# Transformer block with cross-attention and a mixture of experts: seams between stages, and the shared expert's two groups in phases

## The reference

```python
x = x + xattn(_layernorm(x), ctx)     # 16 heads; q, k normalised per head; 496 main keys and
                                      # 16 further keys, each with its own softmax; ctx @ Wo + bo
x = x + moe(_layernorm(x))            # router picks 2 of 7 experts for a row
# every expert, and one shared expert that takes all rows:
u = xt @ Wup + bup
g = silu(u @ Wgate + bgate) * u
out = g @ Wdown + bdown
```

## Time and profile before

| what | value |
|---|---|
| time, median of 3 runs | 1103.38 us (1101.81 to 1104.4) |
| the profiled execution | 1103.13 us; span 1101.3 us |
| PE busy | 976.3 us, 89% of the span |
| ACT busy | 501.8 us, 46% |
| DVE busy | 607.6 us, 55% |
| POOL busy | 686.0 us, 62% |
| mean granted TensorE clock | 0.957 of 2.4 GHz |
| stage project | 0.3 to about 181 us |
| stage attend | 182.5 to 476.4 us |
| stage output | 477.7 to about 633 us |

### The profile page before, as it was taken

One profiled execution on the slowest core, in us unless ns is written; L12 is line 12 of the kernel. 1 busy time (PEld: TensorE's weight loads), 2 busy tenths in 40 slices (PEclk: granted clock), 3 DMA queues, 4 the chain that ended last, 5 costly groups with the idle time before them and its releaser, 6 DMA issues. The chain is left out here.

```text
span 1101.3 us, 17337 instructions
## 1 busy us (share of the span) xinstructions
PE 976.3 (89%) x5217; PEld 443.2 (40%) x5218; DVE 607.6 (55%) x1074; ACT 501.8 (46%) x894; POOL 686.0 (62%) x601
## 2 busy tenths in 40 slices
PE   1789993999999999959988779999999999999898
PEld 1345541222222222226643235544454455554343
DVE  5777773587887877637754323333234333222288
ACT  2466663577877877622242123333333333333340
POOL 1464565479889998742317478989899997000470
PEclk9889996599999999979999889999999999999999
DMA  7135444234343321023426534344334432113674
GB/s 252 34 100 158 118 123 147 72 123 148 130 150 126 115 86 48 20 81 125 134 87 230 199 125 135 116 133 133 112 119 139 143 122 90 57 57 144 240 199 155
DMA packets 89035, 138.26 MB, mean 126 GB/s; under 512 B 9209, under 2 KB 48121, under 8 KB 88593
## 3 DMA queue, kind: packets, MB, share of 16 engines
q1 hardware_dynamic: 74752, 91.07, 25.0%
q0 software_dynamic: 12896, 45.10, 12.4%
q10 hardware_dynamic: 1328, 1.36, 0.4%
HBM read 84.03 MB, written 53.48 MB: 125 GB/s over the span
## 5 line engine op out<-in xcount | busy, mean ns | idle before, releaser
L934 DVE TENSOR_REDUCE nm<-a_psS 128x2 bf16<-128x992 f32 x128 | 152.3, 1190 | 77.1 <-PE a_psS L945 75.6
L871 ACT ACTIVATE p_t<-a_psT 128x512 f32<-128x512 f32 x256 | 143.4, 596 | 36.6 <-PE a_psT L961 34.6
L1716 PE MATMUL e_psU<-w_exp,e_xT 128*128 x456 | 112.6, 383 | 7.5 <-issue 5.7
L1716 PE MATMUL e_psY<-w_exp,e_gT 128*128 x456 | 110.6, 379 | 3.5 <-issue 2.3
L1716 PE MATMUL e_psG<-w_exp,e_uT 128*128 x456 | 110.8, 379 | 2.5 <-DVE e_uT L1683 2.5
L961 PE MATMUL a_psT<-q_stk,k_stk 98*128 98x512 f16 x256 | 101.3, 401 | 5.8 <-ACT p_t L871 5.8
L945 PE MATMUL a_psS<-k_stk,q_stk 96*128 96x512 f16 x256 | 81.7, 402 | 22.7 <-DVE nm L935 13.8
L830 POOL TENSOR_TENSOR p_sum<-p_t,p_t 128x512 f32<-128x512 f32 x64 | 81.3, 1270 | 29.4 <-ACT p_t L871 24.2
L191 POOL TENSOR_TENSOR w_exp<-e_raw,w_exp 128x1024 f32 (+1 forms) x42 | 90.3, 2149 | 6.0 <-POOL e_raw L188 4.5
L1697 DVE TENSOR_TENSOR e_g<-e_g,e_u 128x512 f32<-128x512 f32 x38 | 48.6, 1279 | 80.9 <-ACT e_g L1676 80.9
L833 POOL TENSOR_TENSOR p_sum<-p_sum,p_t 128x512 f32<-128x512 f32 x64 | 81.4, 1272 | 17.0 <-ACT p_t L871 10.7
(11 more groups left out here) (323 smaller groups left out, 1919.1 us busy)
## 6 DMA issues: line engine op xcount, KB each, us to landing
xs_dram<-zero SPq DMA_DIRECT2D x38, 256.0 KB, 5.6
e_x<-xs_dram SPq DMA_DIRECT2D x38, 256.0 KB, 2.7
ys_dram<-e_y SPq DMA_DIRECT2D x38, 256.0 KB, 2.1
q_dram<-q_st SPq DMA_DIRECT2D x24, 256.0 KB, 2.9
k_dram<-k_st SPq DMA_DIRECT2D x24, 256.0 KB, 3.9
q_stk<-q_dram SPq DMA_DIRECT2D x64, 96.0 KB
k_stk<-k_dram SPq DMA_DIRECT2D x64, 96.0 KB
e_raw<-in_L_ffn_Wup_dram POOLq DMA_DIRECT2D x12, 512.0 KB, 4.0
```

Source lines behind the costliest of these rows:

```text
L871: act.activation(probs(w, k), psT[:, k % 2], ACT.Exp, scale=SCALE / (QS * QS)).then_inc(s["exp"], 1)
L934: dve.tensor_reduce(pair[:, :, 0:1].rearrange("p q o -> p (q o)"), psS[:, :, 0:NMAIN], AX.X, ALU.max, negate=True)
L1716: ins = pe.matmul(dst[:, :], stationary, moving, start=(k == 0 and chunks[0] == 0), stop=(k == len(terms) - 1 and chunks[-1] == KD - 1))
```

## The change

It moves work between stages and changes an order; no arithmetic is added or left out.

1. The last pair's six stores of q and k are issued at the head of attend by SP, not at the end of project. `q_st`, `k_st` keep their addresses. ACT, before its first write of split weights (head 8), waits for all stores.
2. After the last head's loads, SP fetches rows 0 to 127 of x and bo (to 128 partitions) into `a_raw`. In output POOL's first instruction adds the two into `x_in[0]`, and ACT's first copies bo into its own tile. `load(0)` and bo's load go away; POOL makes its constants after that addition, and DVE's two copies of them move from before tile 0 to tile 4.
3. ACT's first square root is a dummy one, so the table is loaded at once; the two scalings of the experts' biases go from ahead of tile 0 to behind the square root of tile 4.
4. The shared groups run phase by phase: up 0, up 1, gate 0, gate 1, down 0, down 1 (before: up 0, gate 0, up 1, down 0, gate 1, down 1). `u`, `uT` and `gT` get a second copy, in three quarters of `xT_all` that are free by then; the one that is stored to `xT_dram` has its own semaphore for it, and ACT waits for it before `up(1, 0)`. `prefix` goes from behind gate(0, 1) to behind up(1, 3). DVE does all eight `down` behind the preparation of `pmat`.

In project and attend:

```diff
-            store(sp, B - 1, TB - 1)
...
+            pair = TB // PAIR - 1
+            for buf, dst, done, parts in ((g_["q_st"], q_dram, g_["qk_stored"][0], (0, 0, 1)), (g_["k_st"], k_dram, g_["qk_stored"][1], (0, 1, 0))):
+                for r, part in enumerate(parts):
+                    d = dst[r, (B - 1) * D:B * D, pair * PAIR * P:(pair + 1) * PAIR * P]
+                    sp.dma_start(d.rearrange("(c p) t -> p c t", p=P), buf[:, pair, part]).then_inc(done[pair], 16)
             for u in range(N):
...
+            sp.wait_ge(g_["split_done"], len(early) + 1)
+            sp.dma_start(raw[:, 0, :], t["x"].rearrange("b s d -> (b s) d")[0:P, :]).then_inc(g_["x0_loaded"], 16)
+            sp.dma_start(raw[:, 1, :], t["L0_xattn_bo"].partition_broadcast(P)).then_inc(g_["bo_loaded"], 16)
...
+                    if n == 0 and j == 0:
+                        for q in g_["qk_stored"][0] + g_["qk_stored"][1]:
+                            act.wait_ge(q, 3 * 16 * NT // PAIR // 2)
                     g_["scale_half"](act, raw[:, :, :], raw_ld, n + 1, k, half, m, n, j)
```

In output, SP, POOL and ACT:

```diff
-            load(0)
-            sp.dma_start(bo[:, :], t["L0_xattn_bo"].partition_broadcast(P)).then_inc(s["bo_loaded"], 16)
             load(1)
+            load(2)
             sp.dma_start(wr[:, :, :], t["L0_ffn_Wr"].rearrange("(k p) n -> p k n", p=P)).then_inc(s["r_loaded"], 16)
-            load(2)
...
+            pool.wait_ge(g_["x0_loaded"], 16)
+            pool.wait_ge(g_["bo_loaded"], 16)
+            pool.tensor_tensor(x_in[:, 0], g_["a_raw"][:, 0, :], g_["a_raw"][:, 1, :], ALU.add).then_inc(s["xb_r"], 1)
...
-            act.wait_ge(s["b_loaded"], 16 * 8)
-            act.activation(bias_hi[:, :, :], bias_raw[:, :, :], ACT.Copy, scale=WS).then_inc(s["b_16"], 1)
-            act.activation(bias_16[:, :, :], bias_raw[:, :, :], ACT.Copy, scale=WS).then_inc(s["b_16"], 1)
+            act.wait_ge(g_["bo_loaded"], 16)
+            act.activation(bo[:, :], g_["a_raw"][:, 1, :], ACT.Copy).then_inc(s["bo_copied"], 1)
+            act.activation(sqrt_first[:, :], ident[:, 0:1], ACT.Sqrt)
...
+                if n == TB:
+                    act.wait_ge(s["b_loaded"], 16 * 8)
+                    act.activation(bias_hi[:, :, :], bias_raw[:, :, :], ACT.Copy, scale=WS).then_inc(s["b_16"], 1)
+                    act.activation(bias_16[:, :, :], bias_raw[:, :, :], ACT.Copy, scale=WS).then_inc(s["b_16"], 1)
...
             for c in range(KD):
                 up(0, c)
+            for c in range(KD):
+                up(1, c)
             act.wait_ge(s["exp_in"], 1)
             act.activation(ex[:, :, :], sel[:, :, :], ACT.Exp).then_inc(s["exp"], 1)
...
+            for grp in range(2):
+                for c in range(KD):
+                    gate(grp, c)
+                    if c:
+                        gated_hi(grp, c - 1)
+                gated_hi(grp, KD - 1)
```

In output, DVE (its eight `down` go from ahead of the probabilities and behind `pmat` to behind `pmat`) and PE:

```diff
+                if n == TB:
+                    dve.wait_ge(s["iota"], 2)
+                    link(dve.tensor_copy(ramp[:, :], ramp_i[:, :]))
+                    link(dve.tensor_copy(bidx[:, :], bidx_i[:, :]))
+                    dve.wait_ge(s["bo_copied"], 1)
...
             up_low(0, 3)
+            up_low(1, 0)
+            up_low(1, 1)
+            up_low(1, 2)
 
             dve.wait_ge(s["prefix"], 1)
...
             dve.tensor_copy(slot[:, :, :], slot_f[:, :, :]).then_inc(s["slots"], 1)
+            up_low(1, 3)
...
-            for j in range(TB):
-                down(0, j)
...
+            for j in range(TB):
+                down(0, j)
             for j in range(TB):
                 down(1, j)
...
             up(0, 2)
             up(0, 3)
-            gate(0, 0)
-            gate(0, 1)
-            prefix()
-            gate(0, 2)
-            gate(0, 3)
             for c in range(KD):
                 up(1, c)
+            prefix()
+            for c in range(KD):
+                gate(0, c)
+            for c in range(KD):
+                gate(1, c)
             for j in range(TB):
                 down(0, j)
-            for c in range(KD):
-                gate(1, c)
             for j in range(TB):
                 down(1, j)
```

More of the change, by code:

```diff
@@ L153, in build @@
         zero = nc.alloc_sbuf_tensor_at("zero", [P, D], F32, offset=O_AT + (B - 1) * KD * 2 * S * 2)
+        half_sb = Map(nc, SBUF_LO, V_AT)
+        q_st = half_sb("q_st", [P, 2, 2, CH, PAIR * P], F16)
+        k_st = half_sb("k_st", [P, 2, 2, CH, PAIR * P], F16)
+        HALVES_AT = half_sb.at
         STK_AT = SBUF_LO + E_EARLY * PER_E
@@ L162, in build @@
         qk_stored = [[sem(f"{x}_stored{k}") for k in range(2)] for x in "qk"]
+        x0_loaded = sem("x0_loaded")
+        bo_loaded = sem("bo_loaded")
         stk_loaded = [sem(f"stack_loaded{n}") for n in range(SLOTS)]
@@ L746, in attend @@
     LAST = N + LAG + 4
-    sb = Map(nc, g_["STK_AT"] + 2 * SLOTS * S * 2, g_["O_AT"])
-    raw = sb("a_raw", [P, 2, D], F32)
+    raw = g_["a_raw"]
+    sb = Map(nc, g_["STK_AT"] + 2 * SLOTS * S * 2 + 2 * D * 4, g_["O_AT"])
     nm = sb("nm", [P, 2, TB, 2], BF16)
@@ L1024, in output @@
     xn2 = low("xn2", [P, NT, D], F32)
+    XT_AT = low.at
     xT_all = low("xT_all", [P, B, KD, 2, S], F16)
@@ L1056, in output @@
     mid = Map(nc, g_["O_AT"], g_["V_AT"])
-    u = mid("f_u", [P, KD, S], F32)
-    uT = mid("f_uT", [P, KD, 2, S], F16)
+    XT = KD * 2 * S * 2
+    again = [Map(nc, XT_AT + b * XT, XT_AT + (b + 1) * XT) for b in range(3)]
+    u = [mid("f_u0", [P, KD, S], F32), again[0]("f_u1", [P, KD, S], F32)]
+    uT = [mid("f_uT0", [P, KD, 2, S], F16), again[2]("f_uT1", [P, KD, 2, S], F16)]
     g = mid("f_g", [P, KD, S], F32)
-    gT = mid("f_gT", [P, KD, 2, S], F16)
+    gT = [mid("f_gT0", [P, KD, 2, S], F16), again[1]("f_gT1", [P, KD, 2, S], F16)]
     sb = Map(nc, g_["V_AT"], g_["WO_AT"])
@@ L1157, in _ @@
                 sp.wait_ge(x1_st[k], 16 * ((NT - 1 - k) // 3 + 1))
-            sp.wait_ge(xT_st, 16 * (B // 2))
+            for q in xT_st:
+                sp.wait_ge(q, 16)
             for q in y_st:
@@ L1171, in _ @@
                                pattern=[[1, P]], channel_multiplier=-1).then_inc(s["const1"], 1)
-            pool.wait_ge(s["bo_loaded"], 16)
-            for n in range(NT):
-                pool.wait_ge(x_ld[n % 3], 16 * (n // 3 + 1))
+            for n in range(1, NT):
+                if n == 1:
+                    pool.wait_ge(s["bo_copied"], 1)
+                pool.wait_ge(x_ld[n % 3], 16 * (n // 3 + (n % 3 > 0)))
                 pool.tensor_tensor(x_in[:, n % 3], x_in[:, n % 3], bo[:, :], ALU.add).then_inc(s["xb_r"], 1)
@@ L1243, in gated_hi @@
                 act.wait_ge(s["g_r"], KD * grp + c + 1)
-                at_least(act, s["d_mm"], TB * grp)
-                act.activation(gT[:, c, 0, :], g[:, c, :], ACT.Copy).then_inc(s["g_h"], 1)
+                act.activation(gT[grp][:, c, 0, :], g[:, c, :], ACT.Copy).then_inc(s["g_h"], 1)
             act.wait_ge(s["col_loaded"], 32)
@@ L1249, in _ @@
                 up(0, c)
+            for c in range(KD):
+                up(1, c)
             act.wait_ge(s["exp_in"], 1)
             act.activation(ex[:, :, :], sel[:, :, :], ACT.Exp).then_inc(s["exp"], 1)
-            for c in range(KD):
-                gate(0, c)
-            for c in range(KD):
-                up(1, c)
-                gated_hi(0, c)
-            for c in range(KD):
-                gate(1, c)
-            for c in range(KD):
-                gated_hi(1, c)
+            for grp in range(2):
[4 more added lines that the diff above has]
+                gated_hi(grp, KD - 1)
         @block.vector
@@ L1389, in _ @@
             dve.tensor_copy(slot[:, :, :], slot_f[:, :, :]).then_inc(s["slots"], 1)
-            gated(0, 0)
-            gated(0, 1)
-            gated_low(0, 0)
-            gated(0, 2)
-            gated_low(0, 1)
-            gated(0, 3)
-            gated_low(0, 2)
-            gated_low(0, 3)
+            up_low(1, 3)
             for c in range(KD):
-                up_low(1, c)
+                gated(0, c)
+                if c:
+                    gated_low(0, c - 1)
+            gated_low(0, KD - 1)
             link(dve.tensor_tensor(cmpb[:, :, :], bidx[:, :].unsqueeze(2).broadcast_to([P, NBLK, E - 1]),
@@ L1495, in gate @@
                 at = slice(c * P, (c + 1) * P)
-                product(chunk_bank("g", grp, c), [(weight(1, y, q)[:, at], uT[:, q, x, :]) for q in range(KD)
+                product(chunk_bank("g", grp, c), [(weight(1, y, q)[:, at], uT[grp][:, q, x, :]) for q in range(KD)
                                                   for x, y in ((0, 0), (1, 0), (0, 1))]).then_inc(s["g_mm"], 1)
@@ L1502, in down @@
                 at = slice(j * P, (j + 1) * P)
-                product(chunk_bank("d", grp, j), [(gT[:, q, x, at], weight(2, y, q)) for q in range(KD)
+                product(chunk_bank("d", grp, j), [(gT[grp][:, q, x, at], weight(2, y, q)) for q in range(KD)
```

44 lines of the change are left out of this document (19 added, 25 removed).

## The result

| | before | after |
|---|---|---|
| median of four runs, us | 1102.60 (1101.07 to 1104.40) | 1088.12 (1086.47 to 1088.84) |
| profiled execution, us | 1103.13 | 1086.47 |
| its span, us | 1101.3 | 1084.9 |
| mean granted clock | 0.957 | 0.962 |
| PE busy, share of the span | 89% | 89% (968.5 us) |

The ratio of after to before is 0.9866, with a 95% interval of 0.9846 to 0.9886. That is 14.5 us, or 1.3%, faster. The forecast was 1085.0 with a range of 1080.5 to 1091.5, and the chance of faster was 0.94.

A forecast was written before the change was run, and what follows sets the result against it. PE bound most tiles, with SP's issuing, a chain behind residual 0 and PE's stops at the seams, and scatters beside PE limiting phase order. -3.3 - 6.2 - 9.1 = -18.6 us from 1103.13 gave 1084.5, stated as 1085; range 1080.5 to 1091.5.

The forecast's parts named there:

- Part 1: Seam from project to attend: scores wait for POOL's last low part, not SP's store issues; -3.3 us.
- Nothing gained or lost: Attend's first heads: the clock had begun to fall before the seam, so the shorter stand changes nothing; 0 us.
- Parts 2 and 3: Head of output: earlier residual 0 and a clock that stays up give -7.2, delayed scalings +1.0; sum -6.2 us.
- The +1.0 us for the scalings behind square root 4: Output: ACT's 2.0 us of scalings against 1.06 us of cover make PE wait once for nT; bounds 0 and 2.0.
- Part 4: Shared groups: PE runs through without its stops, and the stage then ends with the scatters; -9.1 us.
- sets what phase order can bring: Shared groups: the slot and scatter chain beside PE, not shortened by PE's order, ends some ten microseconds ahead of the stage.
- B: Rival, end of output: stores of y take over at landings of 7 to 9 us; whole 1090 to 1098; chance 0.09.
- C: Rival, end of output: scatters stretch while VectorE works; all 32 +17 us, in all 1102; half 1093; chance 0.06.
- D: Rival, end of output: y landings make it slower, sum turning at 10.4 us; at 12 us 1110; chance 0.03.
- E: Rival, output: clock drops at its head despite the short wait, and DVE holds back the phases; 1089; chance 0.10.
- F: Rival, end of output: the stage ends with PE, not with the scatters; 1076; chance 0.02.
- Cold either way: Later stages, routed on: PE stands before them either way, so they start cold as before; no change.

The follow-up runs named there:

- the dense version: Changed kernel plus unread matmuls, 10 at the end of project and 3 or 2 beside scores in attention's first seven heads; 1122.25 us, ratio to before 0.9744.
- the first chip: Conditions of the first comparison, taken for a separate chip: kernel before 1102.60 us, changed kernel 1088.12 us.
- the chips of the experiments: Two chips of the follow-up runs, where every kernel is slower; kernel before 1154.73, 1151.27 and 1151.64 us, medians of the three groups.
- third group: Last group of follow-up runs, on the second of their chips; unedited changed kernel 1126.95 us, ratio 0.979 to the kernel before (median 1151.64 us).

## Why the prediction was right, and where it was not

**Part 1, -3.3 forecast, -3.35 measured.** The first scores start 1.17 us after POOL's last low part; 1.3 was forecast. With the stores alone put back, 3.25 us return. What the stores do in attend (4.2 us of SP's queue, ACT's wait at head 8) can't be seen in attend's length: 296.29 us with the stores back, 294.95 to 295.95 in the ten traces of the changed attention with its clock left as it is.

**Attend's own length, 0 forecast, +0.75 measured.** "Nothing gained or lost" was argued from a clock that had fallen before the seam, and it had. The step leaves out that the clock's return within attend is an event of its own. The stretch from 214 to 216 us, of before and then of after:

```profile
214.00:216.00 2.00, 2.00 (x14) 0.60 (x6) 0.35 (x2) 0.33 (x2) 1.27 (x1) 0.52 0.30 104
```
```profile
214.00:216.00 2.00, 2.00 (x13) 0.51 (x12) 1.08 (x2) 0.91 (x2) 0.95 (x1) 0.88 0.02 6
```

In this pair the clock returned at nearly the same time of the axis, although attend began 3.35 us sooner in after, so more work lay at half clock. But that isn't what the change does. With the stores back, attend begins where it did before (182.53), but the clock is back only at 218 us, and attend takes 296.29. In the run with the scalings split, attend begins at 179.30, the clock is back by 212 us, and attend takes 294.95:

```profile
216.00:218.00 2.00, 2.00 (x8) 0.50 (x10) 0.89 (x1) 1.36 (x3) 1.00 (x1) 0.50 0.12 46
218.00:220.00 2.00, 2.00 (x16) 0.45 (x12) 0.65 (x3) 0.76 (x3) 0.27 (x1) 0.90 0.07 11
```
```profile
212.00:214.00 2.00, 2.00 (x20) 0.59 (x14) 0.89 (x1) 1.62 (x3) 0.52 (x2) 0.99 0.18 66
```

In all 13 traces without matmuls added in attend the clock returns some 33 to 36 us after the first scores, wherever the stores stand, and attend is the longer the later it returns. That the low clock costs attention some 5 us is shown by the dense version. That the +0.75 is this change's is not shown, and these runs speak against it: the changed attention took between 294.95 and 295.95 us, and the kernel before took 295.20 and 295.56.

**Parts 2 and 3, -6.2 forecast, -6.1 measured.** All three signs came: residual 0 released by PE, PE's wait for xn 0.20 us (0.5 forecast), tile 2 in 2.75 us. The chain's share and the clock's were both needed: putting back the scalings and the table alone brings 3.99 us of standing, the low clock and 4.3 us net. The +1.0 us for the scalings behind square root 4 was measured as +0.98, taken away by splitting them, and taken away again by moving them back. Bounds 0 and 2.0 were wider than needed. Nothing showed for DVE's two casts or for SP's queue.

**Part 4, -9.1 forecast, -8.8 measured.** Step by step: PE from up 0 to its end takes 64.84 us and had 82.71, that is 17.9 less (17.5 to 18.5 forecast from the three stops and the slow clock), without one wait, and at clock 1.00 to its last matmul. `slot` comes 30.59 us after up 0, where 31.14 - 0.7 = 30.4 was forecast. The 31 steps took 39.83 us, 40.0 forecast. From the last issue to routed's first load it took 5.82 us against 5.2: the one term that was mis-sized. The last scatters landed in busier queues (share 0.98, had 0.99 but only for a part of the time), and the median landing rose from 2.8 to 3.4 us; over the last 19 scatters it was 4.8. So 17.9 us of PE turned into 8.8, since the scatters were next: the reading that "sets what phase order can bring" was right. It rests on this one trace of the first chip, since on the chips of the experiments PE ended the stage. The last scatter's issue came 40.8 us behind `slot`, where 41 to 42 stood among the signs.

**The rivals.** B, the stores of y: their landing rose from a median of 2.4 to 4.2 us, the longest stayed at 5.2, and the last addition came 5.4 us ahead of the last scatter. It was not near. C, scatters stretched by VectorE: each took 0.96 to 1.20 us, and the 31 steps were no longer than before. By the rule of the Trainium skill (SBUF — State Buffer, "SBUF: two separate sides") GpSimd is kept from writing descriptors while VectorE holds the port pair that they share; this trace shows none of it for these scatters, with VectorE at work beside them. Whether any of VectorE's operations here took that pair isn't shown. D's landing of 10.4 us was never seen. E is refuted by 0.20 us and 2.75 us. F, the stage ending with PE, which was given 0.02, is true on the other chips and false on the first: there PE ended 12.3 us ahead of the first load.

**Routed, +1.02, and late, +0.04.** PE stands 14.93 us ahead of routed's first block and not 5.96, and in this trace the block's nine matmuls take 4.05 us against 2.96. "Cold either way" holds for the level, but how soon the clock comes back within the block differs from run to run: first transposes to second took 9.18 us here, 8.07 in before, and 7.74 to 9.05 in the eleven other traces in which PE stood some 6 us ahead of it. Only keeping PE busy gives another value, 5.95. So most of this 1.0 us can be scatter between runs. After is the only trace with the long stand, and its block is the longest, so a small part that comes from the stand can't be ruled out.

The prediction named a change of attend's or routed's own length as a sign that it was wrong. Both changed in this pair, by 0.75 and 1.02 us. By the other traces changes of this size come without any edit, so the sign was set too sharp.

The sum came out right because each term did. The forecast of 1085 is 3.1 us under the median. Of that 1.65 is the profiled execution being the fastest of its four (1088.12 - 1086.47). The other 1.5 is what the stages missed, 2.1 us, less 0.7: 0.5 between the sum for the profiled execution (1084.5) and the rounded 1085, and 0.2 that lie outside the span. The 2.1 are 0.75 in attend, 1.06 from routed on and 0.3 in part 4, with the rest under 0.1; the terms of the change itself are within 0.3 us each. In both stretches the profiled execution of after lies at the long end: its attend is the longest of the ten with the changed attention, and its first block the longest of thirteen. So these two misses are near the largest that the runs show.

## What to carry to other kernels

When PE's stops are taken out of a stage, look first for the chain that runs beside it. Of 17.9 us only 8.8 were to be had here, and by the trace the chain's start (the prefix product) is the next lever. Moving it brought `slot` 6.9 us forward and kept 3.1 to 3.3 us where PE was the bound; where the scatters are, it wasn't run. A clock that has fallen has a price of its own in thin work behind a seam, and cheap unread matmuls can buy it back, as the 5 us in attend show; the same ahead of a stage whose start waits for them lost time. An operation moved off one chain lands on another: put it where the next engine has as much slack as the operation is long, or cut it to that length.

## What the runs showed of the hardware that was not expected

On the chips of the experiments PE got single matmuls at 1.4 or 2.1 us each while POOL's indirect DMAs were under way, 17.0 us of waiting (third group, changed kernel) that nothing in the profile ends. On the first chip the same code had no such wait, at a DMA share of 0.97 where the others had 0.60. It isn't full queues, then, and not the low clock either: the matmuls themselves took 0.58 us, the rest is gaps. In the experiments' twelve traces it began 18 to 25 us after the first scatter (in the third group's changed kernel PE was still at full speed from 550 to 588 us). It ended 3 to 5 us after the last one was issued, also when half of them were left out. DVE and ACT stood too ("issue", "remote"), and late, with POOL's gathers, took 97.6 to 101.2 us instead of 73. That the scatters bring it about is shown by leaving half out: the waits fell from 17.0 to 2.1 us, and the stage by some 22 us. Why is open: that the engines' instruction streams come slowly then is a guess, and the queues of kind "instruction" carry too little in either case (a packet or two in that stretch) to say it. It matters for this change: on such chips the change is worth 15.0 us in this stage (the order alone 10.8 by medians, 13.5 by two traces), because what it ends earlier is PE's work, and PE's work is the bound there.

The granted clock comes back at different moments in the same code. In attend's head it returned between 212 and 215 us of the span where the first scores came at 179.2 to 179.9, and between 215 and 219 where they came at 182.5 to 182.7. It was up by 190 us only where PE had been given more work, in the dense version. Attend's length followed it, by 1.3 us between the extremes (294.95 to 296.29). In routed's first block it moves that block by 1.4 us between runs (7.74 to 9.18). A difference of a microsecond in such a stage, in one pair of traces, can't be told from this.
